# Two transformer layers on one core: three new orders in attention, at the turn between batches, in the last four blocks with the first FFN's begin, and for two sums of moduli

## The reference

```python
q = rms_norm(ln(x) @ wq); k = rms_norm(ln(x) @ wk)       # 16 heads, 4 heads
k_ctx = rms_norm(ctx @ wk_ctx); v_ctx = ctx @ wv_ctx; v = ln(x) @ wv
probs = softmax(rope(q) @ concat(k_ctx, rope(k)).T / sqrt(128) + mask)
x = x + (probs @ concat(v_ctx, v)) @ wo
gamma = mean(abs(w)) + 1e-5; wt = clip(round(w / gamma), -1, 1) * gamma   # w1 and w2
h = square(relu(quant8(ln(x)) @ wt1.T)); x = x + quant8(h) @ wt2.T
x = x + layer1_attention(ln(x), ctx)
x = x + bitlinear(rms(silu(ln(x) @ wg) * (ln(x) @ wu)), wd)
```

## Time and profile before

| what | value |
|---|---|
| time, median of 3 runs | 1585.82 us (1583.65 to 1586.09) |
| profiled execution, its own time | 1588.14 us |
| profiled execution, span of the core | 1586.8 us |
| PE busy | 1509.5 us, 95% of the span |
| DVE, ACT, POOL busy | 1138.8, 991.6, 694.0 us (72, 62, 44%) |
| mean granted TensorE clock | 0.992 of full speed |
| attention's blocks | 26 to 883 us, the first FFN from about 895 us |

### The profile page before, as it was taken

One profiled execution on the slowest core, in us unless ns is written; L12 is line 12 of the kernel. 1 busy time (PEld: TensorE's weight loads), 2 busy tenths in 40 slices (PEclk: granted clock), 3 DMA queues, 4 the chain that ended last, 5 costly groups with the idle time before them and its releaser, 6 DMA issues.

```text
span 1586.8 us, 26709 instructions
## 1 busy us (share of the span) xinstructions
PE 1509.5 (95%) x8887; PEld 1175.4 (74%) x8887; DVE 1138.8 (72%) x2966; ACT 991.6 (62%) x2502; POOL 694.0 (44%) x832
## 2 busy tenths in 40 slices
PE   7999999999999999999998899999997899999988
PEld 5778888888888888888886566666664666666653
DVE  6787777777777777777777645555556888888774
ACT  5666655666666566566666765566666666667655
POOL 5554555554645555546465200000004455555444
PEclk9999999999999999999999999999999899999999
DMA  7011111111111111111335766666664301111000
GB/s 274 27 60 48 41 67 40 53 55 40 61 48 41 68 41 51 56 42 54 120 119 212 266 227 215 218 217 218 219 198 162 106 21 53 48 54 41 28 14 28
DMA packets 50537, 156.73 MB, mean 99 GB/s; under 512 B 5600, under 2 KB 5728, under 8 KB 48992
## 3 DMA queue, kind: packets, MB, share of 16 engines
q1 hardware_dynamic: 50400, 155.02, 27.6%
HBM read 113.05 MB, written 41.94 MB: 98 GB/s over the span
## 4 chain that ended last, share of the span: by engine, by line
PE 73%; DVE 13%; ACT 5%; issue 3%; DMA 3%; POOL 2%; SPq 0%; ACTq 0%; DVEq 0%; POOLq 0%
PE bank L1278 10%; PE bank L337 10%; PE bank L367 9%; PE bank L420 9%; PE quad L407 5%; PE quad L1842 4%; PE quad L1307 3%; PE bank L1332 3%; PE bank L1869 3%; PE quad L395 2%; PE quad L397 2%; PE quad L396 2%; PE bank L1749 2%; PE bank L379 2%; PE bank L1809 1%
## 5 line engine op out<-in xcount | busy, mean ns | idle before, releaser
L616 ACT ACTIVATE Pt<-Pt,small 128x384 f32<-128x384 f32 (+1 forms) x256 | 172.7, 682 | 118.0 <-DVE small L855 117.9
L420 PE MATMUL bank<-PT,vv 128*128 128x512 f32 x672 | 199.2, 405 | 10.3 <-DVE PT L840 7.0
L367 PE MATMUL bank<-wq,xT 128*128 128x512 f32 x768 | 206.9, 404 | 1.7 <-ACT wq L533 0.9
L1088 POOL TENSOR_SCALAR Pt<-Pt,small 128x384 f32<-128x384 f32 (+1 forms) x256 | 164.7, 657 | 87.0 <-DVE small L863 86.9
L1278 PE MATMUL bank<-wq,ot 128*128 128x512 f32 x768 | 191.6, 402 | 2.2 <-DVE xr L1461 2.2
L855 DVE CUSTOM_DVE_ANT_0 Pt<-quad,mask,small 128x384 f32<-128x384 f32 (+1 forms) x256 | 171.3, 680 | 29.0 <-PE quad L397 27.7
L840 DVE TENSOR_TENSOR PT<-quad,PT 128x512 fp32r<-128x512 f32 x224 | 154.0, 688 | 40.1 <-ACT PT L608 39.5
L1278 PEld LDWEIGHTS bank<-wq,ot 128*128 128x128 f32 x768 | 144.2, 191 | 34.8 <-issue 2.8
L367 PEld LDWEIGHTS bank<-wq,xT 128*128 128x128 f32 x768 | 136.7, 189 | 27.3 <-DVE wq L750 2.1
L1076 POOL TENSOR_TENSOR t<-t 128x512 f32<-128x512 f32 x64 | 85.0, 1328 | 140.0 <-DVE t L821 139.9
L420 PEld LDWEIGHTS bank<-PT,vv 128*128 128x128 f32 x672 | 116.4, 189 | 34.3 <-DVE PT L840 15.3
(11 more groups left out here) (278 smaller groups left out, 3558.6 us busy)
## 6 DMA issues: line engine op xcount, KB each, us to landing
ot_scratch<-OT SPq DMA_DIRECT2D x64, 512.0 KB, 2.9
ot<-ot_scratch SPq DMA_DIRECT2D x64, 512.0 KB, 3.4
wkv_f<-in_w SPq DMA_DIRECT2D x12, 512.0 KB, 6.0
wkc_f<-in_w SPq DMA_DIRECT2D x12, 512.0 KB, 6.8
wkv_f<-in_wg SPq DMA_DIRECT2D x11, 512.0 KB, 5.1
wkv_f<-in_wd SPq DMA_DIRECT2D x11, 512.0 KB, 5.0
wkv_f<-in_wu SPq DMA_DIRECT2D x10, 512.0 KB, 4.5
stg<-in_ctxT SPq DMA_DIRECT2D x16, 256.0 KB, 3.3
```

Of the source, the lines that this page charges most:

```text
L367: ins = pe.matmul(bQ[:], xT[p][:, k, qt * 128:qt * 128 + 128], wq[j][:, g, k, :], start=(part == 0 and k == 0), stop=(part == 2 and k == 3))
L420: ins = pe.matmul(bO[:], vv[x][:, bg % 2, kt, :], PT[y][:, k % 2, :], start=(kt == 0 and n == 0), stop=(kt == tiles_in(i) - 1 and n == 2))
L616: act.activation(p, p, ACT.Exp, bias=nm[:, i % 2, h:h + 1], scale=-1.0, accum_out=sm[:, i % 2, h:h + 1]).then_inc(f["s_exp"], 1)
L1088: pool.tensor_scalar(p, p, ri[:, i % 2, h:h + 1], 1.0, ALU.mult, ALU.mult).then_inc(f["p_n"], 1)
```

## The change

At the turn, `pe_kv` goes ahead of the first `pe_x_turn`; the second tile of x is transposed into bank bQ for every batch, so it waits for the queries' rotation and squares in place of the first tile's split; DVE's `v_lo` goes to the end of the block before, ahead of `dve_ln_b` of the first tile, and `dve_ln_b` of the second behind two `dve_ev`; `dve_co` goes from the end of block 15 into the middle of block 16. The `w1` sums go to two other slots of a block: behind `dve_k_ss`, and behind `dve_q_lo` (odd) or ahead of `dve_q` (even). In blocks 61 to 64 the sums of `w2`, the pieces of `wo`, the splits of probabilities and the ternary pieces stand in another order. `pe_keep` of five before the FFN is gone, `pe_y(0, 3)` goes ahead of `pe_w2_sum`, `dve_norm(0)` goes to the head of DVE's FFN program, and the ternary pieces of `w2` and layer 1's first loads are spread otherwise over tiles 0 and 1. All of the arithmetic stays.

```diff
@@ -168,7 +168,7 @@
...
-        return bQ if m == 1 else bT
+        return bQ if m % 2 else bT
@@ 
...
             sp_w2_sums(1)
-        if i >= 63:
-            ffn["sp_w2"](i - 63)
         if i == 64:
...
                 ffn["sp_ot"](c)
+        if i >= 63:
+            ffn["sp_w2"](i - 63)
@@ 
...
         elif m > 1:
-            pe.wait_ge(f["xt_lo"], m)
+            pe.wait_ge(f["q_rope"], 4 * (m - 1))
+            pe.wait_ge(f["q_sq"], 4 * (m - 1))
         for k in range(4):
@@ 
...
         pe_s(i, 1)
+        pe_kv(i + 2)
         if i % 8 == 6 and i + 2 < NBLK:
             pe_x_turn(2 * (i // 8) + 2)
-        pe_kv(i + 2)
         if i == 64:
@@ 
...
         if i > 56:
-            for p in {(57, 0): (0,), (58, 0): (1,), (59, 0): (2,), (60, 0): (3,), (61, 0): (4,), (62, 0): (5,),
+            for p in {(57, 0): (0,), (58, 0): (1,), (59, 0): (2,), (60, 0): (3,), (61, 0): (4,), (62, 1): (5,),
                       (63, 0): (6,), (63, 1): (7,)}.get((i, half), ()):
                 act_wo(p)
-            for q in {(60, 1): (0, 1), (61, 1): (2, 3), (63, 1): (4,), (64, 0): (5, 6), (64, 1): (7,)}.get((i, half), ()):
+            for q in {(61, 1): (0,), (61, 2): (1,), (62, 0): (2,), (62, 1): (3,), (63, 1): (4,), (64, 0): (5, 6),
+                      (64, 1): (7,)}.get((i, half), ()):
                 act_w2_abs(q)
@@ 
...
             act_w_hi(2 * i + 6)
-        act_last(i, 0)
+        if i < 61:
+            act_last(i, 0)
         act_exp(i, 0)
-        if turn:
-            act_x_hi(2 * (i // 8) + 2)
         act_exp(i, 1)
...
         if turn:
+            act_x_hi(2 * (i // 8) + 2)
             act_x_hi(2 * (i // 8) + 3)
-        act_exp(i, 2)
-        act_p_hi(i - 1, 2)
+        if i < 62:
+            act_exp(i, 2)
+            act_p_hi(i - 1, 2)
+        else:
+            act_p_hi(i - 1, 2)
+            act_exp(i, 2)
+        if i == 64:
+            act_last(i, 0)
         if i in (2, 4):
             act_w_hi(2 * i + 7)
-        act_exp(i, 3)
-        act_p_hi(i - 1, 3)
+        if i < 62:
+            act_exp(i, 3)
+            act_p_hi(i - 1, 3)
+        else:
+            act_p_hi(i - 1, 3)
+            act_exp(i, 3)
         act_k_hi(i + 2)
         act_q_hi(i + 1)
+        if i == 62:
+            act_last(i, 0)
+        if i == 64:
+            act_last(i, 1)
         act_o(i - 1)
         act_v_hi(i + 2)
-        act_last(i, 1)
+        if i == 62:
+            act_last(i, 1)
         if i % 8 == 4 and i + 4 < NBLK:
@@ 
...
             act_w_hi(2 * i + 6)
-        act_last(i, 0)
         if i > 1:
             act_k_sq(i + 2)
+        act_last(i, 0)
         act_exp(i, 2)
...
         act_q_hi(i + 1)
+        if i == 61:
+            act_last(i, 1)
         act_o(i - 1)
...
         act_k_hi(i + 2)
+        if i == 61:
+            act_p_hi(61, 0)
         act_v_hi(i + 2)
-        act_p_hi(i, 0)
-        act_last(i, 1)
+        if i != 61:
+            act_p_hi(i, 0)
+        act_last(i, 2 if i == 61 else 1)
@@ 
...
             dve_w1_gamma()
-        for q in {(62, 0): (0,), (62, 1): (1,), (63, 0): (2,), (63, 1): (3,)}.get((i, half), ()):
+        for q in {(62, 1): (0,), (63, 1): (1,)}.get((i, half), ()):
             if q == 0:
@@ 
...
         turn = i % 8 == 6 and i + 2 < NBLK
-        dve_v_lo(i + 1)
-        dve_ev(i, 0)
-        dve_p_lo(i - 1, 0)
-        dve_ev(i, 1)
-        dve_o_lo(i - 2)
+        if not turn and i != 62:
+            dve_v_lo(i + 1)
+        if i < 62:
+            dve_ev(i, 0)
+            dve_p_lo(i - 1, 0)
+            dve_ev(i, 1)
+            if turn:
+                dve_ln_b(2 * (i // 8) + 3)
+            dve_o_lo(i - 2)
+        else:
+            if i == 64:
+                dve_p_lo(63, 0)
+            dve_ev(i, 0)
+            dve_ev(i, 1)
+            if i == 62:
+                dve_v_lo(i + 1)
+            if i == 64:
+                dve_o_lo(i - 2)
         if i in (2, 4):
             dve_w(2 * i + 5)
-        dve_last(i, 0)
-        if turn:
-            dve_x_lo(2 * (i // 8) + 2)
         dve_q_ve(i + 1)
...
         if i == NBLK:
-            mem["dve_ternary"](0, 4)
+            mem["dve_ternary"](0, 2)
         dve_ri(i, 0)
         dve_k_ss(i + 2)
+        dve_last(i, 0)
+        if i == 16:
+            dve_co()
+        if turn:
+            dve_x_lo(2 * (i // 8) + 2)
+        dve_ev(i, 2)
         if turn:
             dve_x_lo(2 * (i // 8) + 3)
-        dve_ev(i, 2)
+        if i == 62:
+            dve_p_lo(i - 1, 2)
         dve_ev(i, 3)
...
         dve_k_n(i + 2)
-        dve_p_lo(i - 1, 2)
+        if i != 62:
+            dve_p_lo(i - 1, 2)
+        if i == 62:
+            dve_p_lo(i - 1, 3)
         dve_ri(i, 1)
-        dve_p_lo(i - 1, 3)
+        if i == NBLK:
+            mem["dve_ternary"](0, 3)
+        if i != 62:
+            dve_p_lo(i - 1, 3)
+        if i == NBLK:
+            mem["dve_ternary"](0, 4)
         dve_k_lo(i + 2)
...
             dve_w(2 * i + 7)
+        dve_last(i, 1)
         dve_q(i + 2)
-        dve_last(i, 1)
@@ 
...
         dve_q_lo(i + 1)
+        dve_last(i, 1)
         if i in (1, 3):
...
             dve_ln_a(2 * (i // 8) + 3)
+        if i == 61:
+            dve_o_lo(60)
         dve_k_lo(i + 2)
+        if i == 61:
+            dve_p_lo(61, 0)
         dve_q(i + 2)
         if prep:
+            dve_v_lo(i + 2)
             dve_ln_b(2 * (i // 8) + 2)
-            dve_ln_b(2 * (i // 8) + 3)
-        if i == 15:
-            dve_co()
-        dve_last(i, 1)
@@ 
...
     def pe_program():
-        mem["pe_keep"](quad[:, 0, :], 5)
+        pe_y(0, 3)
         pe_w2_sum()
-        pe_y(0, 3)
         pe_y(1, 0)
@@ 
...
             mem["act_ternary"](0, q)
-        act.wait_ge(f["w_gamma"], 4)
-        act_w2(2)
         for n in range(NT):
...
             if n == 0:
+                act.wait_ge(f["w_gamma"], 4)
+                act_w2(2)
                 act_w2(3)
                 act_w2(4)
-                act_w2(5)
+            if n == 1:
+                act_l(1)
             if n == NT - 1:
@@ 
...
             if n == 0:
+                act_w2(5)
                 act_w2(6)
                 act_w2(7)
+            if n == 1:
+                act_l(2)
             for j in range(2):
...
             if n < NT - 2:
-                for k in range(3) if n == 0 else range(max(ends[n], 3), ends[n + 1]):
+                for k in range(1) if n == 0 else range(max(ends[n], 3), ends[n + 1]):
                     act_l(k)
@@ 
...
     def dve_program():
+        dve_norm(0)
         dve.wait_ge(f["w_sum"], 2)
         mem["dve_gamma"](1, bM[:, 0:8])
-        mem["dve_ternary_clip"](0, 5)
-        mem["dve_ternary_clip"](0, 6)
-        dve_norm(0)
-        mem["dve_ternary_clip"](0, 7)
-        mem["dve_ternary_clip"](1, 2)
+        for q in (5, 6, 7):
+            mem["dve_ternary_clip"](0, q)
         dve_w2(0)
@@ 
...
             if n == 0:
-                for q in (3, 4, 5):
+                for q in (2, 3, 4):
                     mem["dve_ternary_clip"](1, q)
@@ 
...
             if n == 0:
-                for q in (6, 7):
+                for q in (5, 6, 7):
                     mem["dve_ternary_clip"](1, q)
...
             if n < NT - 2:

```

## The result

The changed kernel takes 1567.81 us (median of 4 runs, 1566.98 to 1568.57), the kernel before in the same session 1585.95 (4 runs, 1583.65 to 1589.25): a ratio of 0.9886, 95% interval 0.9873 to 0.99. The profiled execution took 1567.12 us with a span of 1565.8. The prediction was 1567, with 1560.5 to 1575 as its range.

What follows compares the result with a forecast made beforehand. PE, busy for 95% of the span, was taken to bound the kernel, so time could come only from its waits, half-clock stretches or work. Terms 5.8 + 1.8 + 3.3 + 8.7 = 19.6 us gave 1567, range 1560.5 to 1575.

Steps and rivals of the forecast that it cites:

- Turn: Seven turn blocks: `pv` starts at 5.22 in place of 6.05, 0.83 us a turn, 5.8 in all, bounds 0 to 10.4.
- Rival B: The turn gives its full 1.49 us: 1562, or 1560 with no fall of the clock; chance 0.12.
- Coefficient chain: Moved from the end of block 15 into block 16, it no longer delays `v_lo`: 1.8 us, bounds 1.2 and 1.88.
- w1's sums: Blocks 58 to 60: sums of w1's moduli in new slots, mostly hidden in DVE's waits: 3.3 us, from 2 to 4.5.
- Block 63 to the FFN: Block 63 up to `p_turn(63, 0)` from 15.05 to 13.0 us, from there to the FFN's first x transposition 21.89 to 19.55.
- the part on the clock: Blocks 61 to the second tile: one of two clock falls stays, 1.6 us of 10.3, leaving 8.7.
- Tile 0: FFN tile 0 grows from 24.72 to 25.9 us: w2 pieces on ACT and DVE make `hh` 1.2 late.
- Tile 1: FFN tile 1 from 19.85 to 17.2 us: 1.1 from a wait gone, 1.6 from the half clock.
- D: Removed waits come back before the next product, in the turns and the end: within 3.2 us, 1583 to 1589; chance 0.05.
- C: The last blocks give half or less, 4 to 6 us more: 1571 to 1577; chance 0.19.
- A: As forecast, the three parts each give within a third of the sum: 1562 to 1572; chance 0.60.
- E: Slower, by 14 more clock falls than the one counted, behind the new waits: around 1592; chance 0.04.

Runs made afterwards that it cites:

- experiment 4: The changed kernel with DVE's first `ln_b` of a turn moved behind `p_lo(i - 1, 0)`, after POOL's `q_add`: 1560.19 us, ratio 0.9847 to the kernel before.
- experiment 2: The changed kernel with the coefficient chain back at the end of block 15: 1568.99 us in one run.
- experiment 9: The changed kernel with the moves of experiment 4 and experiment 5, ACT's w2 piece 4 after the squares and DVE's clip of it after norm(1): 1560.02 us.
- experiments 6: The kernel before with w1's sums, and the ternary pieces made by the same calls, in their new slots alone: 1583.8 us in one run.
- 7: The changed kernel with all three of layer 1's first loads summed on ACT before tile 1's `act_xq`, as before: 1568.06 us, ratio 0.9886 to the kernel before.
- experiment 5: The changed kernel with `p_hi(63, 3)` ahead of two w2 sums on ACT and `p_lo(63, 3)` ahead of ternary piece 3 on DVE: 1565.32 us, ratio 0.9876.
- 10: The kernel before with only the new orders of blocks 61 to 64 and of the FFN's begin: 1575.55 us in one run.
- experiment 1: The kernel before with the new order of the turn alone: 1581.89 us, ratio 0.9979.

## Why the prediction held, step by step

- **Turn: mechanism right, term too large.** 0.83 a turn was forecast and 4.24 / 7 = 0.61 measured (0.62 by the turn blocks alone). The held `ln_b` ends 2.49 us into the block (2.5 forecast) and `o_lo` starts at 4.55 (4.5). `pv` starts at 5.37, not 5.22: 0.14 pass between the end of `o_lo` and `pv`, which the sum left out. The block gives 0.65 for the 0.68 that `pv` comes earlier. The `ln_b` of 1.4 was as forecast. So the term that was mis-sized is the start of `pv`. Rival B is excluded for this kernel and is what experiment 4 made of it: at 13.17 a turn gives 1.45, for the 1.49 named as the bound.
- **Coefficient chain:** 1.88 for 1.8. In block 16 it takes 1.1 (247.01 to 248.14), for 1.3. What the prediction did not count is that the wait it removes can bring a fall, 1.5 more (experiment 2).
- **w1's sums:** 3.33 for 3.3, blocks 12.29, 13.23 and 13.71 for 12.29, 13.24 and 13.65; the wait of PE for both sums is there, 1.01 before line 429 (428 before the change).
- **Blocks 61 and 62:** 13.23 and 8.70 for 13.24 and 8.9. `s(62, 2)` waits 0.82 for `ev(62, 0)`, where 1.05 was forecast, `pv(61, 3)` and `s(63, 0)` 0.36 and 0.23, where 0.7 and 0.5 were.
- **Block 63 to the FFN:** 12.80 for 13.0, and 20.77 for 19.55. Without a fall the second is 19.25, so the step was 0.3 too long, and the 1.5 more is the one fall that the part on the clock counted by itself. The wait before `pv(63, 3)` was 1.62 for 1.9.
- **Tile 0:** 25.82 for 25.9. The size was right and the reason wrong, which is luck: the sum held ACT's passes and DVE's pieces for the cause, and what made `hh` late is ACT's wait of 1.04 for the load of a piece, which the sum did not have (experiment 9). The cover behind the 16th piece was wider than the 0.8 forecast: its clip ends at 906.23, the first copy of `h` behind it at about 907.3, and `down` starts at 909.37 without a wait. Experiment 9, which makes the piece later and `down` due earlier, used it up, and PE waited 0.48.
- **Tile 1:** 16.94 for 17.2. The 1.1 that the sum gave to the new order was a late load of that one execution: worth 0, 0.66 or 1.33 (experiments 6, 7, before). As a gain of the order it was argued from one trace, and the order's sure part is only that it no longer depends on the later loads. The 1.6 that the sum gave to the half clock came by luck: that fall stands behind a wait which the change leaves as it was, and it came in two of the eight executions with the new order, too.
- **The other rivals:** D is out, since the stages shortened as forecast; only part of the waits came back (1.08 before `kv` as 0.58 before `pv`, and see experiment 5). C is out for the last blocks, 9.75 for 8.7, and without tile 1 6.84 for 6.0. A is what came. E is out, with fewer falls than before and not more.
- **The clock:** one fall of two was to stay in this region, and one stayed, behind the wait of 1.62 that the text had named. But that was luck: with the same wait, experiments 2, 4 and 10 had none, and with the new order experiments 5 and 9 had one in tile 1. The Trainium skill, TensorE: Matmul & The Clock Gate, "HAM oscillation — how this bites in real kernels", tells of a kernel with waits of 3 to 5 us for its transfers, behind each of which the clock is at half again. The waits here are shorter, 1.1 to 2.2, and the same wait brought a fall in some executions only, so the page does not settle the case, and the second fall that the prediction drew from it did not stay in this execution.

The sum came out at 19.55 for 19.6 with two errors of opposite sign: the turns 1.6 too high, the end 1.05 too low (9.75 for 8.7), and 0.35 that belongs to no term. That the two errors cancel is luck, and so are the falls: an execution with one in tile 1, or with none before the FFN, is 1.6 longer or 1.5 shorter with the same kernel. What the experiments bear out is the mechanism of the turn, of the chain and of the slots. What stays open is what decides whether a wait of 1.1 to 2.2 us brings a fall, and why the loads of tile 1 land when they do.

## What to carry to other kernels

When an order is changed so that two engines no longer wait in turn, look for operations of VectorE that now start beside one of GpSimd: here moving one of 0.54 us by two places in its queue was worth 0.8 us at each of seven places, more than the whole new turn order gave. Price a wait from when the next group could have started, not from the idle time that the profile writes, and expect the wait to come back at the next consumer of the same engine (1.62 to 0.16, then 0.75 to 1.43). A gain that stands on a load's landing or on a fall of the clock should be told apart from one of the order, since another execution may not have it.

## What the runs showed of the hardware

- `ln_b` on 128 x 512 f32 takes 0.54 us alone and 1.40 beside POOL's addition, ending 0.28 behind it. In the new order POOL's addition keeps its 1.29, where in the old one it took 1.50 with an `ln_b` started before it. A `tensor_tensor` of VectorE on 128 x 1 takes 1.00 beside POOL's addition and 0.18 without it.
- The falls of the granted clock to 1.2 GHz in these traces are 3.41 or 6.83 us long, but for one cut off by the end of the program. One of 3.41 cost 1.5 to 1.6 where PE was busy (block 16 of experiment 2: 15.66 for 14.17; the changed kernel's 20.77 for 19.25 before the FFN; tile 1: 18.52 for 16.92), and nothing where PE would wait (block 62 of experiment 1: 10.76 at 0.84, 10.77 at 1.00).
- Falls stood behind waits of PE of only 1.1 to 2.2 us, and the same wait brought one or none: 1.62 before the last `pv` a fall in the changed kernel and none in experiment 4; 1.13 and 0.34 in tile 1 none in the changed kernel and a fall in experiment 5; 2.02 in block 62 none before and a fall in experiment 1.
